# Routing tables of two expert layers: operands in the rounded f32 format, weights in two parts, built eight picks at a time

## What is computed

```
# first expert layer, per token
route = softmax(x @ router_w + router_b)
out = y[argmax(route)] * max(route)
# second expert layer, per token
k_logits, k_index = top_k(logits, 2)
k_prob = softmax(k_logits)
out = sum over both picks of k_prob * h[k_index]
x = x + tanh(g_ffn[l]) * out
```

## Time and profile before

| | us |
|---|---|
| median of 3 runs | 1360.92 (1360.55 to 1364.99) |
| the profiled execution | 1368.55 |
| its span | 1366.8 |
| TensorE busy | 1180.5 |
| VectorE busy | 520.4 |
| ScalarE busy | 465.5 |
| GpSimd busy | 479.6 |

### The profile page before, as it was taken

One profiled execution on the slowest core, in us unless ns is written; L12 is line 12 of the kernel. 1 busy time (PEld: TensorE's weight loads), 2 busy tenths in 40 slices (PEclk: granted clock), 3 DMA queues, 4 the chain that ended last, 5 costly groups with the idle time before them and its releaser, 6 DMA issues.

```text
span 1366.8 us, 19293 instructions
## 1 busy us (share of the span) xinstructions
PE 1180.5 (86%) x7110; PEld 863.4 (63%) x7110; DVE 520.4 (38%) x1256; ACT 465.5 (34%) x1067; POOL 479.6 (35%) x496
## 2 busy tenths in 40 slices
PE   2466799999995889999999999999948999998986
PEld 2246699999993444545445454434438888888875
DVE  1574322221114796767667676522060010000100
ACT  2111122221110245555555555663302333333331
POOL 0150111111113156767557675580002333333322
PEclk9885699999996689999999999999957999999998
DMA  6114487878862000000000000012005999999984
GB/s 202 50 62 154 170 292 277 292 291 305 325 251 100 0 1 1 1 17 1 1 1 17 1 1 16 9 39 101 0 0 196 317 306 315 294 308 302 330 299 124
DMA packets 53978, 197.18 MB, mean 144 GB/s; under 512 B 8539, under 2 KB 34397, under 8 KB 38013
## 3 DMA queue, kind: packets, MB, share of 16 engines
q1 hardware_dynamic: 39584, 173.35, 35.7%
q0 software_dynamic: 10464, 18.36, 5.5%
q10 hardware_dynamic: 3836, 4.24, 1.0%
HBM read 179.54 MB, written 16.38 MB: 143 GB/s over the span
## 4 chain that ended last, share of the span: by engine, by line
PE 66%; DMA 14%; DVE 10%; issue 4%; ACT 3%; POOL 1%; SPq 1%; ACTq 0%; POOLq 0%; DVEq 0%
PE PQ L394 16%; DMA out<-Z,SI 10%; PE PB L408 10%; PE PB L499 7%; PE PQ L484 7%; PE PB L468 5%; PE PQ L538 4%; PE PB L279 4%; PE PB L489 4%; DVE Z L872 3%; PE PQ L468 2%; DMA Z<-xn,SI 2%; PE PB L359 2%; DVE SM L585 1%; PE PQ L279 1%
## 5 line engine op out<-in xcount | busy, mean ns | idle before, releaser
L394 PE MATMUL PQ<-Z,WS 128*128 128x128 f32 x2720 | 329.4, 278 | 13.7 <-issue 12.6
L394 PEld LDWEIGHTS PQ<-Z,WS 128*128 128x128 f32 x2720 | 324.6, 194 | 26.1 <-issue 19.6
L408 PE MATMUL PB<-WS,Z 128*128 128x256 f32 x992 | 237.1, 383 | 0.0
L872 DVE TENSOR_REDUCE Z<-PB 128x1 f32<-128x402 f32 x340 | 183.4, 567 | 87.1 <-PE PB L468 85.8
L408 PEld LDWEIGHTS PB<-WS,Z 128*128 128x128 f32 x992 | 180.6, 192 | 19.9
L484 PE MATMUL PQ<-QS,KS 128*128 128x512 f32 x416 | 173.1, 437 | 7.3 <-ACT Z L1082 4.5
L1020 ACT ACTIVATE Z<-PQ,WS 128x128 f32<-128x128 f32 x312 | 88.9, 368 | 208.7 <-PE PQ L394 208.7
L468 PE MATMUL PB<-KS,QS 128*128 128x402 f32 x340 | 132.6, 402 | 15.6 <-DVE Z L872 6.8
L484 PEld LDWEIGHTS PQ<-QS,KS 128*128 128x128 f32 x416 | 77.1, 190 | 105.0 <-issue 60.8
L1082 ACT ACTIVATE Z<-PQ 128x512 f32<-128x512 f32 x208 | 109.7, 604 | 86.2 <-PE PQ L484 86.0
L1082 ACT ACTIVATE WS<-PQ 128x512 f32<-128x512 f32 x208 | 109.3, 605 | 80.6 <-PE PQ L484 80.6
(11 more groups left out here) (242 smaller groups left out, 1213.1 us busy)
## 6 DMA issues: line engine op xcount, KB each, us to landing
WS<-in_w SPq DMA_DIRECT2D x62, 1024.0 KB, 6.7
WS<-in_w SPq DMA_DIRECT2D x23, 2048.0 KB, 7.9
WS<-in_w SPq DMA_DIRECT2D x39, 1028.0 KB, 7.5
Z<-in_b SPq DMA_DIRECT2D x39, 128.0 KB, 6.7
xn<-WS SPq DMA_DIRECT2D x32, 128.0 KB, 1.7
X<-in_x SPq DMA_DIRECT2D x4, 512.0 KB, 10.7
WS<-yd SPq DMA_DIRECT2D x4, 512.0 KB, 5.5
out<-X SPq DMA_DIRECT2D x4, 512.0 KB, 2.9
```

Source lines behind the costliest of these rows:

```text
L394: t = e.matmul(bank[:, j * P:j * P + P], w[:, k, o:o + P], FXT[i % 2][:, k * P:k * P + P], start=k == 0, stop=k == 1)
L408: t = e.matmul(y, FS[c % 4][:, j * P:j * P + P], w[:, 4 * n + j, :], start=n == 0 and j == 0, stop=n == 1 and j == 3)
L872: e.tensor_reduce(MP[j % 2][:, i:i + 1], PB[bank_of["pc", r]][:, 0:PIECE], AX.X, ALU.max).then_inc(v_pc, 1)
```

## The change

- `lanes` and `vals` move to KS, in the rounded f32 format. Since that format keeps fewer bits, the weights are split: `prh` is the rounded weight and `prl` what is left, each with its own columns in `vals`; the table's read adds them. Rows and one-hots are small whole numbers. The moving operand gets 3 x 24 = 72 columns in the first layer and 3 x 40 = 120 in the second, where it had 46 and 78. One tile number more is added so that widths are even.
- `hot`, `vals` and `lanes` are made for eight chunks of picks, then for the next eight.
- The increment of `v_oh` moves from the scaled weights to the one-hots, so `ranks` does not wait for the softmax.
- GpSimd's gathers wait for `tabi` alone, and the first down projection waits for `tabp`.

```diff
+        KSW = KS.rearrange("p h k -> p (h k)")
+        prh, prl = KSW[:, 8192:8192 + 2 * NC], sm(2 * NC)
...
-            nt, cc = (NT0, NT1)[l], NC * (1 + l)
-            lanes = WS[1][:, 4096 - cc * P:4096].rearrange("p (q n) -> p q n", n=P)
-            hot = WS[1][:, 4096:4096 + cc * nt].rearrange("p (q t) -> p q t", t=nt)
-            vals = (WS[1][:, 4608:4608 + 2 * cc * nt] if l == 0 else VW[:, 0:2 * cc * nt])
-            return lanes, hot, vals.rearrange("p (q s t) -> p q s t", s=2, t=nt)
+            n, cc = (NT0, NT1)[l] + 1, NC * (1 + l)
+            lanes = KSW[:, 0:cc * P].rearrange("p (q n) -> p q n", n=P)
+            hot = WS[1][:, 4096:4096 + cc * n].rearrange("p (q t) -> p q t", t=n)
+            vals = KSW[:, 4096:4096 + 3 * cc * n].rearrange("p (q s t) -> p q s t", s=3, t=n)
+            return lanes, hot, vals
...
-                e.wait_ge(v_oh[l], 1)
+                e.wait_ge(v_oh[l], 1 + l)
...
-                    t = e.matmul(PB[6][:, 0:2 * nt], lanes[:, q, :], vals[:, q, :, :].rearrange("p s t -> p (s t)"),
+                    t = e.matmul(PB[6][:, 0:3 * nt + 3], lanes[:, q, :], vals[:, q, :, :].rearrange("p s t -> p (s t)"),
...
+                        if i == 0:
+                            e.wait_ge(v_tab[l], 2)
...
-                    vc.step(e, e.tensor_tensor(oh[:, k * NC:(k + 1) * NC, :], iota,
-                                               tt.unsqueeze(2).broadcast_to([P, NC, E]), ALU.is_equal))
+                    e.tensor_tensor(oh[:, k * NC:(k + 1) * NC, :], iota,
+                                    tt.unsqueeze(2).broadcast_to([P, NC, E]), ALU.is_equal).then_inc(v_oh[l], 1)
+                    e.wait_ge(v_oh[l], k + 1)
...
-                e.tensor_scalar(pr[:, 0:cc], pr[:, 0:cc], tg[:, 2 + l:3 + l], None, ALU.mult).then_inc(v_oh[l], 1)
+                vc.step(e, e.tensor_scalar(pr[:, 0:cc], pr[:, 0:cc], tg[:, 2 + l:3 + l], None, ALU.mult))
+                vc.step(e, e.tensor_copy(prh[:, 0:cc], pr[:, 0:cc]))
+                e.tensor_tensor(prl[:, 0:cc], pr[:, 0:cc], prh[:, 0:cc].bitcast(F32), ALU.subtract)
...
-                vc.step(e, e.tensor_tensor(hot, CT[:, C_IOT:C_IOT + nt].unsqueeze(1).broadcast_to([P, cc, nt]),
-                                           tile[:, 0:cc].unsqueeze(2).broadcast_to([P, cc, nt]), ALU.is_equal))
...
-                e.scalar_tensor_tensor(vals[:, :, 0, :], row[:, 0:cc].unsqueeze(2).broadcast_to([P, cc, nt]),
-                                       float(P - 1), hot, ALU.add, ALU.mult)
-                e.tensor_tensor(vals[:, :, 1, :], hot, pr[:, 0:cc].unsqueeze(2).broadcast_to([P, cc, nt]), ALU.mult)
                 for q in range(0, cc, 8):
-                    e.tensor_tensor(lanes[:, q:q + 8, :], iota128.unsqueeze(1).broadcast_to([P, 8, P]),
-                                    lane[:, q:q + 8].unsqueeze(2).broadcast_to([P, 8, P]), ALU.is_equal).then_inc(v_slot[l], 1)
+                    part = slice(q, q + 8)
+                    wide = [P, 8, nt + 1]
+                    vc.step(e, e.tensor_tensor(hot[:, part, :], CT[:, C_IOT:C_IOT + nt + 1].unsqueeze(1).broadcast_to(wide),
+                                               tile[:, part].unsqueeze(2).broadcast_to(wide), ALU.is_equal))
+                    e.scalar_tensor_tensor(vals[:, part, 0, :], row[:, part].unsqueeze(2).broadcast_to(wide),
+                                           float(P - 1), hot[:, part, :], ALU.add, ALU.mult)
+                    for k, half in ((1, prh.bitcast(F32)), (2, prl)):
+                        e.tensor_tensor(vals[:, part, k, :], hot[:, part, :],
+                                        half[:, part].unsqueeze(2).broadcast_to(wide), ALU.mult)
+                    e.tensor_tensor(lanes[:, part, :], iota128.unsqueeze(1).broadcast_to([P, 8, P]),
+                                    lane[:, part].unsqueeze(2).broadcast_to([P, 8, P]), ALU.is_equal).then_inc(v_slot[l], 1)
...
-                e.tensor_copy(tabp[:, 0:nt], PB[6][:, nt:2 * nt]).then_inc(v_tab[l], 1)
+                vc.step(e, e.tensor_copy(tabp[:, 0:nt], PB[6][:, nt + 1:2 * nt + 1]))
+                e.tensor_tensor(tabp[:, 0:nt], PB[6][:, 2 * nt + 2:3 * nt + 2], tabp[:, 0:nt], ALU.add).then_inc(v_tab[l], 1)
...
-                e.wait_ge(v_tab[l], 2)
+                e.wait_ge(v_tab[l], 1)
```

More of the change, by code:

```diff
@@ L35 @@
 C_N = 1354
-SMN = 3048
+SMN = 3080
 def constants():
```

## The result

The changed kernel takes 1354.16 us (median of 7 runs, 1352.7 to 1358.63). The kernel before, timed beside it, takes 1364.99 (7 runs, the three of above among them). The ratio is 0.9933, 95% interval 0.9915 to 0.9952: 9.1 us less, between 6.5 and 11.6. The profiled execution took 1355.98 us, its span 1354.2; before it was 1368.55 and 1366.8.

The account below looks back on a forecast made before the run. Both expert stages, one bound by TensorE and one by transfers, were taken to start only behind a table. Gains of 3.8 and 7.5 us sum to 11.3, giving 1349.6 us from the 1360.92 median; range 1346 to 1356.5.

Parts of the forecast that it names:

- The sum: Whole kernel: 3.8 us gained at the first table and 7.5 at the second, 11.3 in all.
- rivals on columns and clock: Table matmuls pay full f32 column price, 8.0 us gained (30%); or TensorE's clock rises later, 7.3 gained (6%).
- One sign that the prediction named: Forecast is wrong if the span from the table's read to the end changes by more than 2 us.
- The price of a narrow rounded matmul: Table matmuls on TensorE: one record of 218 ns a pick in place of 436, columns hidden behind the weights.
- The argument from the equal weight loads: TensorE weight loads, rounded 190 ns and f32 194 at 128 columns, so a rounded pick goes at the f32 record's pace.
- The shorter load of the Trainium skill: Table weight loads at 107 ns for 128 columns: 12.9 us gained in place of 11.3; chance 5%.
- columns-at-full-price rival: Table matmuls: format halves weights, not columns; a pick costs 0.25 or 0.42 us, 8.0 us gained, 1352.9; chance 30%.
- the one in which the format buys nothing: Table matmuls stay at 436 ns a pick; ranks and split in eights gain 4.8 us, 1356.1; chance 10%.
- The ranks: Ahead of each table, ranks wait for the one-hots, not the softmax: 0.93 us gained in the first, 1.47 in the second.
- VectorE's groups: Eight picks on VectorE take 2.33 us in the first table and 2.85 in the second, where VectorE sets the pace.
- The tail: Behind the first table, the two-step weights delay the mask chain, whose flag releases the first transpose: 0.20 us lost.
- The clock: Rival: TensorE's clock rises some 4 us later, losing half of that in each stage; 7.3 us gained, 1353.6; chance 6%.

Follow-up runs that it names:

- e3: Changed kernel with only the groups of eight undone: hot and value columns for all picks first, then the comparisons; ratio 0.9922.
- e8: Changed kernel plus unread 512-column f32 matmuls in TensorE's idle stretches, six ahead of the first table, two behind it, four behind the second; 1352.87 us, ratio 0.9898.
- e4: Changed kernel with the mask chain and its two small matmuls moved ahead of the first table; ratio 0.9899.
- e4b: Second run of the changed kernel with the mask chain moved ahead of the first table; ratio 0.9922.
- e5: Changed kernel with the two weight-column multiplications for each eight picks moved from VectorE to GpSimd; ratio 0.9934.
- e7: Changed kernel with table matmuls in plain f32 on 48 and 80 columns, low parts of the weights left out of the result; ratio 0.9936.
- e2: Changed kernel with only the format of the table's matmuls undone: plain f32, still 72 and 120 columns; ratio 0.9944.
- e9: Changed kernel with early mask chain, unread 512-column matmuls around both tables and 256-column ones after each eight picks but the last; 1351.49 us, ratio 0.9896.

## Why the prediction was right

**The sum.** 11.3 us in the steps, 11.2 in the traces' stretches, 9.1 and 13.4 in two timings. Every line of the table above is within 0.1 us of its step. All behind the tables moved with them, as the chain of waits and the bound of either stage had said, but for the clock's share below. TensorE and the transfers are as dense as in the earlier trace rows:

```profile
158.00:418.00 260.00, 256.70 (x1959) 246.21 (x1957) 54.27 (x134) 49.49 (x93) 41.14 (x42) 1.00 0.78 280
1056.00:1336.00 280.00, 256.04 (x1723) 234.00 (x1723) 26.43 (x68) 89.04 (x310) 88.17 (x68) 1.00 0.95 307
```

The times alone would not have shown it. The interval of 6.5 to 11.6 us holds the forecast's 11.3 and also the 8.0 and 7.3 of the rivals on columns and clock, and 1354.16 is nearer to their 1352.9 and 1353.6 than to 1349.6; it is the stretches in the traces that tell them apart. One sign that the prediction named was luck: from the second table's read to the end it took 334.5 us before and 333.3 after, within the 2 us that it allowed, but 331.5 in the second execution of the same changed kernel. A stretch that scatters so can't tell whether the prediction is wrong.

**The price of a narrow rounded matmul**, the step with the least behind it, was taken as 218 ns and measured as 221 by the same count (time over number), 213 from start to start, like an f32 record. The argument from the equal weight loads of 190 and 194 ns held. The shorter load of the Trainium skill (TensorE: Matmul & The Clock Gate, LDWEIGHTS; 107 ns) is not that of these tables: e3's 32 weight loads take 6.90 us back to back at 1.2 GHz. It is close to what the rows show at 2.4 GHz, where the rounded matmuls of e8's first table (eight in 1.08 us) and the f32 records of L394 start 112 ns apart. The section gives the figure without a clock, and the prediction did not ask at which it holds. The columns-at-full-price rival (30%) and the one in which the format buys nothing (10%) fall with e3.

**The ranks** were worth 0.97 and 1.44 us against 0.93 and 1.47; in the first layer bound by the two new operations of VectorE, in the second by TensorE, as put. **VectorE's groups** took 2.33 and 2.87 us against 2.33 and 2.85.

**The tail.** The flag chain still released the first transpose, with 4.07 us behind the read instead of the 3.95 forecast; the read had come 0.07 earlier than forecast, so only 0.05 of this miss is left in the sum. One cast in the chain grew:

```profile
148.25 0.39 DVE L799 CAST MBH<-SM 128x13 fp32r<-128x13 f32 x1
```

It took 0.17 before. It lies beside GpSimd's issue of a gather (147.65 to 148.67), as another slow operation of the chain did before (L788, 0.28 us at 151.32, beside one from 150.62 to 151.64). With the chain ahead of the logits and no gather beside it (e4, e4b) the cast took 0.17 again. In e5 the two engines block each other; that it is the same here was not tested.

**The clock** did take a little back: in the first experts stage the first 32 records of the up projection needed 5.95 us, and the window says

```profile
154.00:158.00 4.00, 4.00 (x25) 4.00 (x25) 0.00 (x0) 0.60 (x1) 0.00 (x0) 0.65 1.01 427
```

The same 32 took 5.28 in the kernel before, so 0.67 us went there, and 1.00 in the second execution of the changed kernel, where they took 6.28. The clock rose 3.0 us behind the first of these records in the kernel before (at 157.9) and 4.5 and 5.2 us behind it in the two of the changed one. The gain at the second transpose of that stage is 3.1 and 2.7 us, where it was 3.75 at the first. In the second stage the second sixteen took 2.24 against 2.18: nothing. The rival had said that the clock would rise later, and in the first stage it did; its 2 us a stage did not come. Its reason, fewer records ahead, is not shown: with as many table records as before the 32 took 5.66 us in e7 and 5.88 in e2, and there is one trace alone of the kernel before. The forecast had put this term at nothing.

**What the parts are worth,** each undone alone, at the two reads: format 6.2 us (2.9 against the f32 matmuls of full width, whose clock rose), ranks 2.4, groups of eight 0.7. That is 9.3 of 11.4; the remaining 2.1 appear only with two of them together. In e3 TensorE starts the second table 4.0 us later (20.09 in place of 16.10) and loses 0.5 by it, because at 221 ns a pick it catches up with VectorE. With f32 operands it could not, and the early start should count for more there; that pair was not run. The prediction did not split the parts so, and gave the groups more weight than e3 leaves them.

## To carry to other kernels

Where one engine produces for another in a chain, compute both paces, not only the one that ends last: here halving TensorE's price moved the bound to VectorE, and the finer interleaving was then worth only 0.7 us. The price of a matmul with few moving columns did not depend on their number here: records of 46 to 120 columns all started 213 ns apart at 1.2 GHz, so going from two records to one halved it, and half as many columns again cost nothing. An idle engine is not a free one: work moved from VectorE to GpSimd made the operations of both longer, and the tables came later. And extra matmuls help only where they reach up to the work: in e8 and e9 they ended 3.40 and 4.07 us ahead of the second table, and the clock was down when it began.

## What the runs showed of the hardware

- In the table with f32 records of 120 columns the granted clock rose from 1.2 to 2.4 GHz, 5.3 us behind the first of them (e2). It stayed at 1.2 GHz over 13.94 us of such records with 78 columns (before) and 80 (e7), at the same pace and with TensorE shown busy all the time. So a TensorE that is busy in the profile is not always one whose clock rises, and a sum must take the level from the rows of its own stretch. That was the one miss among the expectations of the format's price.
- In e8 and e9 the clock was at 2.4 GHz ahead of the second table and fell while TensorE was idle (3.40 and 4.07 us), at 1009.0 and 1010.5, just before the first rounded matmul. Over the table it stayed at 1.2 GHz, in e9 though TensorE was busy throughout.
- Matmuls in the rounded format of 72 and 120 columns started 213 ns apart at 1.2 GHz, and so did the records of f32 ones of 46, 78, 80 and 120 columns, of which each matmul has two. At 2.4 GHz it was 112 ns, for the rounded ones of 72 columns (e8) and for f32 records of 128.
- VectorE's 128x1024 comparison grew from 1.22 to 1.74 us beside GpSimd's multiplications, and each of these (128x320) ended some 0.58 us behind the VectorE operation that it met.
